# Scatter products of an edge pass in shared PSUM banks, added further behind, with one TensorE signal a group

## The reference

```python
def direction(idx, etype, W):            # once for each half of the edges
    row, col = (idx[0], idx[1])
    norm = compute_norm(row, col, n)
    m = ccorr(x[col], rel_full[etype]) @ W    # circular correlation of node and relation
    m = m * norm[:, None]
    return jax.ops.segment_sum(m, row, num_segments=n)
out = (in_res + out_res + loop_res) * (1.0 / 3.0) + bias
out = (out - mu) / jnp.sqrt(var + BN_EPS) * gamma + beta
return (jnp.tanh(out), (rel_full @ w_rel)[:-1])
```

## Time and profile before

| what | us |
|---|---|
| median of 3 runs (lowest, highest) | 3601.29 (3593.56, 3602.86) |
| the profiled execution, its time | 3595.45 |
| its span in the trace | 3593.6 |
| first edge pass, first gather to the last addition | 1216.2 to 2284.0 |
| second edge pass, first gather to the last issue of a gather | 2322.8 to 3379.8 |

### The profile page before, as it was taken

The page is one execution under the profiler, slowest core; times in us unless marked ns, Lnnn a source line. Parts: engine busy times, 40 slices in busy tenths (PEclk is TensorE's granted clock), DMA queues, the critical chain, the costliest instruction groups (busy, mean ns, idle before and its releaser), DMA issues.

```text
span 3593.6 us, 42994 instructions
## 1 busy us (share of the span) xinstructions
PE 1969.8 (55%) x12269; PEld 1526.2 (42%) x12270; DVE 2043.1 (57%) x5268; ACT 1316.1 (37%) x3225; POOL 2381.6 (66%) x2455
## 2 busy tenths in 40 slices
PE   0004777676676665555555555355555555555553
PEld 0002343344343455555555555345545555554421
DVE  5777888886242344444444444467666666666533
ACT  0016666663021243333333433144333333334210
POOL 0177777777777677777777777277777777777400
PEclk9998556556798655555555555588787777778776
DMA  1000000000610222222322221333233422223293
GB/s 35 0 1 1 2 2 2 2 2 3 221 14 4 67 56 53 53 52 54 52 53 53 53 53 45 54 92 81 78 78 78 77 78 79 78 78 78 37 170 59
DMA packets 188975, 191.34 MB, mean 53 GB/s; under 512 B 80863, under 2 KB 160587, under 8 KB 188239
## 3 DMA queue, kind: packets, MB, share of 16 engines
q1 hardware_dynamic: 110243, 104.96, 12.1%
q0 software_dynamic: 78496, 83.60, 11.5%
HBM read 161.27 MB, written 27.09 MB: 52 GB/s over the span
## 4 chain that ended last, share of the span: by engine, by line
POOL 58%; issue 23%; DVE 10%; DMA 3%; SPq 2%; PE 2%; DVEq 2%; ACT 0%; ACTq 0%; PEldq 0%; POOLq 0%
POOL gx L1432 36%; POOL sorted_edges L253 22%; DVE part_prod L1517 3%; DVE acc L1503 2%; SPq L1907 2%; DMA gx<-gather_table,gidx_s 2%; DVE prod L1527 1%; DMA adj_again<-adj_saved 1%; DVE run L385 1%; DVEq L1495 1%; PE psum L1840 0%; DVE rank L388 0%; DVEq L1503 0%; PE psum L1829 0%; DVE oh_t L1489 0%
## 5 line engine op out<-in xcount | busy, mean ns | idle before, releaser
L1432 POOL DMA_INDIRECT gx<-gather_table,gidx_s x1664 | 1600.7, 962 | 573.1 <-issue 501.3
L253 POOL DMA_INDIRECT sorted_edges<-rec,row_i x784 | 778.9, 993 | 423.9 <-issue 258.6
L1544 PE MATMUL psum<-rel_parts,oh_t 128*128 128x96 bf16 (+1 forms) x4992 | 567.8, 290 | 891.2 <-DVE oh_t L1489 445.3
L1466 ACT ACTIVATE sq_s<-cst,lo_s 128x125 f32<-128x125 f32 x1664 | 527.0, 387 | 1193.4 <-PE psum L1558 1183.3
L1544 PEld LDWEIGHTS psum<-rel_parts,oh_t 128*128 128x128 bf16 x4992 | 461.6, 129 | 970.1 <-DVE oh_t L1489 478.6
L1503 DVE TENSOR_TENSOR acc<-acc,psum 125x64 f32 (+1 forms) x1664 | 418.7, 252 | 549.2 <-issue 258.8
L1558 PE MATMUL psum<-prod,oh_s 128*125 128x64 f32 (+1 forms) x3328 | 686.8, 375 | 22.0 <-DVE prod L1527 22.0
L1517 DVE TENSOR_TENSOR part_prod<-gx,psum 128x256 f32<-128x256 f32 (+1 forms) x832 | 423.4, 550 | 404.6 <-DMA gx<-gather_table,gidx_s 392.4
L1558 PEld LDWEIGHTS psum<-prod,oh_s 128*125 128x125 f32 x3328 | 641.1, 287 | 23.9 <-issue 22.9
L624 PE MATMUL psum<-oh_dst,oh_src 128*125 128x500 bf16 x784 | 409.9, 596 | 152.6 <-DVE oh_dst L580 134.2
L591 DVE TENSOR_TENSOR adj<-adj,psum 125x500 f32 x392 | 260.3, 664 | 77.6 <-issue 76.3
(11 more groups left out here) (327 smaller groups left out, 1037.7 us busy)
## 6 DMA issues: line engine op xcount, KB each, us to landing
tb<-sorted_types SPq DMA_DIRECT2D x416, 128.0 KB, 3.1
gx<-gather_table,gidx_s POOLq DMA_INDIRECT x1664, 2.5
adj_saved<-adj SPq DMA_DIRECT2D x1, 17171.9 KB
adj_again<-adj_saved SPq DMA_DIRECT2D x6, 2734.4 KB
sorted_edges<-rec,row_i POOLq DMA_INDIRECT x784, 2.1
gather_table<-scaled SPq DMA_DIRECT2D x12, 224.0 KB
adj_saved<-adj SPq DMA_DIRECT2D x1, 1993.2 KB
adj_again<-adj_saved SPq DMA_DIRECT2D x6, 317.4 KB
```

Source lines behind the costliest of these rows:

```text
L253: nc.gpsimd.indirect_dma_start(rec_d[c // HC], bass.IndirectOffsetOnAxis(ap=row_i[:, c:c + 1], axis=0), rec[:, c, :], None).then_inc(sent. ...
L1432: nc.gpsimd.indirect_dma_start(gx[g % DEEP][:, k, :], None, table_d[d], bass.IndirectOffsetOnAxis(ap=gidx_s[:, t:t + 1], axis=0),).then_in ...
L1466: sq = nc.scalar.activation(sq_s[:, k, :], iota[:, 0:LO], ACT.Square, bias=lo_s[:, t:t + 1], scale=-1.0)
L1544: mm = nc.tensor.matmul(ps_rel[g % RELS_KEPT][:, k * RS:k * RS + W], oh_t[g % (AHEAD + 1)][:, k * P:(k + 1) * P], rel_parts[:, s, :], star ...
```

## The change

In the first pass the scatter products of two groups share a bank, so that four banks hold eight groups. `oh_s` and `prod` become eight deep there, and the additions of a group come six iterations behind its products, not three. As a bank must not be read while TensorE writes it, the additions of a group wait until both groups of its bank are scattered. In the second pass a group fills a bank, and these depths stay as they were. In both passes TensorE no longer signals after the relations, only after the scatter; VectorE's products of group g wait for the scatter of group g - early, ahead of which the relations of g were issued, and for the first `early` groups there is one signal after all of their relations.

```diff
-        BEHIND = 3
...
+            IN_BANK = BANK // (GROUP * d)
+            BEHIND = 4 * IN_BANK - 2 if IN_BANK > 1 else 3
+            OUTS = 4 * IN_BANK
+            SOURCES = 4 * IN_BANK
...
-                oh_s = [sb(f"oh_s{u}", [P, GROUP, LO], F32, c) for u in range(4)]
+                oh_s = [sb(f"oh_s{u}", [P, GROUP, LO], F32, c) for u in range(SOURCES)]
...
-                prod = [sb(f"prod{u}", [P, GROUP, d], F32, c) for u in range(BEHIND + 1)]
+                prod = [sb(f"prod{u}", [P, GROUP, d], F32, c) for u in range(OUTS)]
...
-                ps_out = [psum[0:LO, (4 + u) * BANK:(4 + u) * BANK + GROUP * d] for u in range(BEHIND + 1)]
+                ps_out = [psum[0:LO, 4 * BANK + u * GROUP * d:4 * BANK + (u + 1) * GROUP * d] for u in range(OUTS)]
...
-                            if g >= 4:
-                                act.wait_ge(scat_done.sem, g - 3 + scat_done.base)
+                            if g >= SOURCES:
+                                act.wait_ge(group_done.sem, g - SOURCES + 1 + group_done.base)
...
-                            dve.wait_ge(scat_done.sem, g + 1 + scat_done.base)
+                            dve.wait_ge(group_done.sem, (g // IN_BANK + 1) * IN_BANK + group_done.base)
...
-                                dve.wait_ge(rel_done.sem, g + 1 + rel_done.base)
+                                if g < early:
+                                    dve.wait_ge(rel_done.sem, 1 + rel_done.base)
+                                else:
+                                    dve.wait_ge(group_done.sem, g - early + 1 + group_done.base)
...
-                            mm.then_inc(rel_done.sem, 1)
+                            return mm
 
                         for g in range(early):
-                            relations(g)
+                            mm = relations(g)
+                        mm.then_inc(rel_done.sem, 1)
...
-                            mm.then_inc(scat_done.sem, 1)
+                            mm.then_inc(group_done.sem, 1)
```

More of the change, by code:

```diff
@@ L1415, in gnn_stack @@
         rel_done, mult_done, prod_done = signal("rel_done"), signal("mult_done"), signal("prod_done")
-        scat_done, squared = signal("scat_done"), signal("squared")
+        group_done, squared = signal("group_done"), signal("squared")
         AHEAD = 3
-        BEHIND = 3
         MANY = 4
@@ L1469, in _ @@
                             act.wait_ge(squared.sem, g + 1 + squared.base)
-                            nc.scalar.activation(oh_s[g % 4][:], sq_s[:], ACT.Relu, bias=one_col,
+                            nc.scalar.activation(oh_s[g % SOURCES][:], sq_s[:], ACT.Relu, bias=one_col,
                                                  scale=-2.0).then_inc(oh_s_made.sem, 1)
@@ L1498, in add_group @@
                         def add_group(g, buckets):
-                            dve.wait_ge(scat_done.sem, g + 1 + scat_done.base)
+                            dve.wait_ge(group_done.sem, (g // IN_BANK + 1) * IN_BANK + group_done.base)
                             for k in range(GROUP):
                                 to = acc2[:, bass.ds(buckets[g % MANY * GROUP + k] * d, d)]
-                                link(v.tensor_tensor(to, to, ps_out[g % (BEHIND + 1)][:, k * d:(k + 1) * d], ALU.add))
+                                link(v.tensor_tensor(to, to, ps_out[g % OUTS][:, k * d:(k + 1) * d], ALU.add))
                         link(v.memset(acc, 0.0))
@@ L1526, in _ @@
                                 dve.wait_ge(mult_done.sem, g + 1 + mult_done.base)
-                                v.tensor_tensor(prod[g % (BEHIND + 1)][:], part_prod[:, :, 0, :], part_prod[:, :, 1, :],
+                                v.tensor_tensor(prod[g % OUTS][:], part_prod[:, :, 0, :], part_prod[:, :, 1, :],
                                                 ALU.add).then_inc(prod_done.sem, 1)
@@ L1557, in _ @@
                             for k in range(GROUP):
-                                mm = nc.tensor.matmul(ps_out[g % (BEHIND + 1)][:, k * d:(k + 1) * d], oh_s[g % 4][:, k, :],
-                                                      prod[g % (BEHIND + 1)][:, k, :], start=True, stop=True)
-                            mm.then_inc(scat_done.sem, 1)
-            for s in (mult_done, oh_t_made, oh_s_made, squared, rel_done, prod_done, scat_done):
+                                mm = nc.tensor.matmul(ps_out[g % OUTS][:, k * d:(k + 1) * d], oh_s[g % SOURCES][:, k, :],
+                                                      prod[g % OUTS][:, k, :], start=True, stop=True)
+                            mm.then_inc(group_done.sem, 1)
+            for s in (mult_done, oh_t_made, oh_s_made, squared, prod_done, group_done):
                 s.base += GROUPS
+            rel_done.base += 1
             for u in range(DEEP):
```

## The result

The changed kernel takes 3603.5 us (median of 20 runs, 3598.96 to 3609.9), the kernel before 3597.64 us (20 runs in turn with them, 3593.56 to 3604.52). The ratio is 1.0015, 95% interval 1.0008 to 1.0022: 5.4 us more (0.0015 x 3597.6), where 4.4 were forecast.

A forecast was written before the change was run, and what follows sets the result against it. GpSimd's gathers were taken to bound both passes. Parts 1 and 2 added 0 us and the first pass's tail 4.4, so 3601.3 + 4.4 = 3605.7, rounded to 3606; range 3596 to 3616.

The forecast's parts named there:

- What bounds the kernel: Both passes are as long as GpSimd's gathers, 1.249 us each, plus the way from the last gather to the join.
- Part 1: TensorE raises one count a group, not two; 208 increments fewer in each pass, no instruction saved: 0 us.
- Part 2: VectorE's products wait for scatter g-3 or g-2, done in time, 2.07 us before in the tight second pass: 0 us.
- the 2 us worked out: First pass's start: first products wait for two relation groups more, some 2.0 us, made up later: 0 us.
- Part 3: First pass's tail: 12 more additions after the last gather, 4.35 us; the register load costs nothing new.
- The effect of the load in iteration 206: First pass's end: the register load moves to iteration 206, delaying the last products by 0 to 1.35 us; 0 if profiled.
- The sum: Whole kernel: the runs' median of 3601.3 us plus 4.4 gives 3605.7, rounded to 3606.
- I count them as chance: Ends of both passes: late landings of the last gathers, about 5 us in the first, taken as chance, not forecast.
- GpSimd's long instructions: Gathers starting at a VectorE one-hot take longer: 10.6 us in the first pass, 19.5 in the second; left out of the sum.
- B: Rival: more gathers meet a one-hot in the first pass, 8.9 us more, 3614.6 us; 9%.
- C: Rival: fewer gathers meet a one-hot, three quarters of 30.1 us go, 3583 us, faster; 5%.

The follow-up runs named there:

- E2: Kernel before with only the wait moved: one TensorE signal a group, products waiting for earlier scatters; ratio 0.9999, on a chip where TensorE sets the pace.
- E11: Changed kernel with first-pass additions three groups behind again, shared banks, depths and single signal kept; ratio 0.9995 to the kernel before.
- E10: Kernel before with additions one group behind in both passes and distinct rows in the padding; 3578.39 us against 3605.23, ratio 0.9931.
- E4: Kernel before with the type one-hots made twice, first into spare buffers nobody reads, where TensorE sets the pace; ratio 1.0024.
- E8: Kernel before with the type one-hots made twice, run again where TensorE sets the pace; ratio 1.0014.
- E12: Kernel before with the type one-hots made twice, run where the gathers set the pace; ratio 0.9981.

## Why the prediction was right, point by point

- **What bounds the kernel**: right on the chip predicted for. Gathers of 944 ns and steps of 0.30 us before and after. It is not so on every chip: on two others TensorE was late, and the passes took about a fifth longer from first to last gather (E2).
- **Part 1, fewer signals, 0 us**: right within what was measured (E2 0.9999; E11 at most 0.04% of cost).
- **Part 2, the wait for scatters, 0 us**: right in its price. It took 5.9 us of VectorE's time in the second pass, never at the last products. In the first pass, where the prediction has the scatter done without exception, VectorE waited for it four times, 4.8 us in all, as the backlog of the start was worked off (1259 to 1265 us) and once at 1729.6. The start came later by the 2 us worked out: the first products at 1252.54 behind a wait of 1.30 us for relations, before at 1249.97, 2.57 us, of which 0.7 is the gathers' own later start (1216.9, before 1216.2). It was made up.
- **Part 3, 4.35 us**: right in mechanism, shown by E11, and slightly small. The tail grew by 4.80. The twelve additions took 4.21 us, a little less than their 4.35; the load behind them cost 4.23 us of idle time instead of 3.78, and the sixteen additions after it 6.02 us instead of 5.80. The prediction had said that the load costs nothing new. The effect of the load in iteration 206 was 0 in this trace, as forecast for late landings, but by little: the last products still waited 0.25 us for their gather, where E11's waited 4.26. With gathers that land early it would show.
- **The sum**: +4.4 forecast, +5.4 (2.9 to 7.9) measured. In absolute numbers 3606 against 3603.5, since three runs had put the median of before 3.7 us higher than twenty did. That 4.4 and 5.4 lie close proves little, as the interval is 5 us wide; E11 and the tails carry the mechanism.
- **"I count them as chance"**, the disturbance of the landings: wrong. It was the padding, in every run, and E10 removed it. It did not touch the forecast, as both kernels pay it.
- **GpSimd's long instructions**: the one-hot was the wrong instruction. The gather of the earlier trace rows starts behind the one-hot's end, and the 0.39 us that it takes longer are the wait for the end of the sum; gathers held by a sum made 27.2 us of the 30 above the median, those held by a one-hot 2.9. The prediction charged the one-hots with what the sums cost, and the expectation of a ratio of 1.008 in E4, E8 and E12 fell with it. What rivals B and C needed, a shift of VectorE against the gathers' starts, was right as an idea, and E12 showed it going the way of C. In the change itself the means stayed (956 and 966 ns) and neither rival happened.

## What to carry to other kernels

When one engine's queue is as long as the stage, look at what is left behind its last instruction: each group by which a consumer runs later is paid once, in full, at the join, and gains nothing in the middle. Such a distance is cover against a late engine, so before cutting it ask whether that engine is ever late; here some 12 us of tails were to be had where it was not (by E10's trace), and 2.8% lost where it was. A disturbance that stands at the same instruction in two traces is no chance: ask what data that instruction handles. And when an instruction is lengthened, do not stop at the neighbour that ended just ahead of it: line up its end with the end of what runs beside it.

## What the runs showed that I had not expected

- Gathers whose 128 rows are all one row of the table keep the DMA engines busy at a share of 0.93 for 20 GB/s, against 0.15 for 28 GB/s with distinct rows (windows 2260 to 2265 of before and of E10). The products of a pass's last gather then start 8.6 us after its instruction starts, not 2.7.
- The same program takes 3600 us on some chips and 4883 to 4914 us on others, with TensorE idle for up to 40.9 us at a time with nothing that the profile shows it waiting for.
- Loading 16 registers on VectorE costs 3.8 us of idle time in a tail, and 4.23 when it follows a row of additions; it is as much as ten additions (3.78 / 0.3625). In the tail of the second pass it is 3.51 us in the kernel before.
- A VectorE sum of two SBUF halves lengthened gathers that start in its first 0.27 us, by up to 0.53 us (1.476 us, not 0.944); they end 0.82 us after it.
- A second, useless one-hot a group made the kernel 0.19% faster, by moving that sum off the gathers' starts in one pass.
